# Cross-attention on one Trainium2 core: GpSimd issues the merge of the rest tiles behind the second addition of the next step instead of the first

## The chip, the cores and the metric

The kernel runs on one core of one Trainium2 chip. The metric is the device time of one execution in microseconds. The kernel is written engine by engine: TensorE (PE in the profile, its weight loads PEld), VectorE (DVE), ScalarE (ACT), GpSimd (POOL) and SyncE (SP) each run their own program, and semaphores order them.

## The reference

Cross-attention with grouped queries, on 4 batches of 1024 queries and 1601 keys, width 1024, 32 query heads, 8 key heads (4 query heads share one), head width 32:

```python
q = hidden_state @ Wq + bq          # (4, 1024, 1024)
k = encoder_hidden_state @ Wk + bk  # (4, 1601, 256)
v = encoder_hidden_state @ Wv + bv
scores = einsum('bkgld,bksd->bkgls', q, k) * scale + encoder_attention_mask
attn = softmax(scores, axis=-1)
out = einsum('bkgls,bksd->bkgld', attn, v)
x = out @ Wo + bo + hidden_state
return (x - mean(x)) * rsqrt(var(x) + 1e-6) * gamma + beta
```

Everything is float32. The mask is all zeros in these inputs; the kernel looks at a flag and takes the program without the mask.

## The kernel before

It has three stages with a barrier between them: `project` (queries, keys, values, written to DRAM), `attend`, and `output` (the last projection and the normalisation). The change is in `attend`.

**The steps of `attend`.** There are 64 steps: 8 blocks of 512 queries (`LQ`) by 8 key heads, each for the 4 query heads (`G`) that share a key head. A step has two halves which overlap with its neighbours'. For the *next* step TensorE computes scores with queries as rows (L882), and VectorE takes their maxima (L1027). For *this* step TensorE computes the scores again, transposed and with the maximum taken off (`logit`, L927), for 13 tiles (`ST`) of 128 keys by 4 heads, 52 in all; ScalarE takes their exponents (L1086) into a tile `weights` of 128 keys x 4 heads x 512 queries, 1 MiB; TensorE multiplies each tile with the values into `mixed` (L937).

**The denominators.** The sum of the exponents over all keys is taken in two parts. Nine tiles (`POOL` in the code: 0, 1, 3, 4, 6, 7, 9, 10, 12) are added by GpSimd, in 8 additions (`add`, L802), into `sum_pool`, one buffer for even and one for odd steps. The four others (`REST`: 2, 5, 8, 11) are added by DMAs that accumulate: `add_rest` (L813) adds tile 5, 8 or 11 into the buffer of tile 2. Then one more accumulating DMA, `merge` (L820), adds that buffer into `sum_pool`. All these DMAs are issued by GpSimd, in its own program's order, from one queue. Last, TensorE sums `sum_pool` over the keys with a matrix of ones (`denominators`, also L937, `logit<-sum_pool,ones` in the profile), ScalarE copies the result (L1104), and SyncE stores it. The denominators of step s are computed by TensorE in step s+1.

**The order around the change.** TensorE follows a string written out by hand (`ORDER`) in which each letter is one item: L a logit, S a half of scores, M a tile's mixing, T the turning of the maxima, P the denominators of the step before. P is the 62nd of 99 letters. What stands there waits for `rest_merged`, the merge's semaphore; everything behind it in the string waits with it. GpSimd's order is written in `sums`:

```python
for n in range(NPOOL):
    ...
    for k, st in enumerate(REST):
        if k and POOL[n] < st < POOL[n + 1]:
            add_rest(quad, s, k)
    add(quad, s, n)
    if n == 0 and not first:
        merge(quad * QUAD + (s - 1), s - 1)
```

An addition waits for the exponents of its tile and for the addition before it; `add_rest` for its tile's exponents and for the `add_rest` before it; `merge` for all additions and all rest additions of its step. In turn ScalarE, before it writes a tile, waits until the tile that last used the buffer has been mixed and added: the GpSimd tiles share 4 buffers, tiles 5, 8 and 11 share 2, tile 2 has 2 of its own, which are free when the merge of the step before last has landed.

**The last step** (63) has no scores of a next one. GpSimd leaves out the additions from tile 10 on and the last rest addition; TensorE sums tiles 10 to 12 itself. While it runs, SyncE loads what the output stage needs first: the weights `wo_parts` (L731) and the first `weighted` and `reciprocals` (L101, L106).

Of the kernel before, what the change touches and what calls it, by code (L numbers as in the profile page):

```python
# [527 lines left out]
def attend(nc, mask_flat, q_dram, k_dram, v_dram, a_dram, d_dram, r_dram, wo_dram, ident, flag, qk_store, qk_in, wo_in, mask_store, first_a, first_r, first_in):  # L528
# [14 lines left out]
    FIRST_ORDER = ORDER.replace("S", "SS", 2 * (LEAD - FIRST_LEAD))  # L543
    LO_AT = 24
    assert [ORDER.count(k) for k in "LSMTP"] == [ST * G, 2 * NROW, ST, 1, 1]
    BANKS = 3
    USES = [k for k in ORDER if k in "LTP"]
    assert len(USES) % BANKS == 0
    TURN, SUMS = USES.index("T"), USES.index("P")
# [8 lines left out]
    def bank_before(step, u):  # L558

        while True:  # L560
            u -= BANKS
            if u < 0:
# [10 lines left out]
    def buffer(s, st):  # L573

        if st == REST[0]:
            return s % BASES
        tiles, size, first = ring(st)
        return first + (s * len(tiles) + tiles.index(st)) % size
# [9 lines left out]
    with ExitStack() as held:  # L588
# [22 lines left out]
        score = [held.enter_context(nc.psum_tensor(f"score{i}", [P, 2, 512], F32)) for i in range(2)]  # L611
        logit = [held.enter_context(nc.psum_tensor(f"logit{i}", [P, LQ], F32)) for i in range(BANKS)]
        mixed = held.enter_context(nc.psum_tensor("mixed", [P, LQ], F32))
# [168 lines left out]
        @block.gpsimd  # L782
        def _(pool):

            nc.gpsimd.memset(ones[:], 1.0).then_inc(const_done, 1)
            for i, k in enumerate(k_sb[2:]):
                pool.wait_ge(const_done, 1 + i)
                nc.gpsimd.memset(k[STACK:SHIFT, :].bitcast(F32), 1.0).then_inc(const_done, 1)
            pool.wait_ge(const_done, 3)

            def add(quad, s, n):

                step, st = quad * QUAD + s, POOL[n + 1]
                w = min(P, S - st * P)
                pool.wait_ge(exp_done, quad * (QUAD * ST * G) + (s * ST + st + 1) * G)
                if n == 0:
                    pool.wait_ge(denom_done, step + 1)
                    first = weights[buffer(s, POOL[0])]
                else:
                    pool.wait_ge(pool_added, step * NPOOL + n)  # L800
                    first = sum_pool[s % 2]
                nc.gpsimd.tensor_tensor(sum_pool[s % 2][0:w], first[0:w], weights[buffer(s, st)][0:w], ALU.add).then_inc(pool_added, 1)  # L802

            def add_rest(quad, s, k):

                step, st = quad * QUAD + s, REST[k]
                pool.wait_ge(exp_done, quad * (QUAD * ST * G) + (s * ST + st + 1) * G)
                if k == 1:
                    pool.wait_ge(mix_done, quad * (QUAD * ST) + (s * ST + REST[0] + 1 + MIX0))
                else:  # L810
                    pool.wait_ge(rest_added, step * (16 * (len(REST) - 1)) + 16 * (k - 1))
                pool.sem_inc(pool_seen, 1)
                pool.dma_start(weights[buffer(s, REST[0])][:], weights[buffer(s, st)][:], accum_op=ALU.add).then_inc(rest_added, 16)  # L813

            def merge(step, s):

                pool.wait_ge(pool_added, step * NPOOL + NPOOL)
                pool.wait_ge(rest_added, step * (16 * (len(REST) - 1)) + 16 * (len(REST) - 1))
                pool.sem_inc(pool_seen, 1)
                pool.dma_start(sum_pool[s % 2][:], weights[buffer(s % QUAD, REST[0])][:], accum_op=ALU.add).then_inc(rest_merged, 16)  # L820

            def sums(quad, s, first=False, last=False):
                for n in range(NPOOL):
                    if last and POOL[n + 1] >= LATE:
                        break
                    for k, st in enumerate(REST):
                        if k and POOL[n] < st < POOL[n + 1]:
                            add_rest(quad, s, k)
                    add(quad, s, n)
                    if n == 0 and not first:  # L830
                        merge(quad * QUAD + (s - 1), s - 1)

            any_mask = pool.value_load(flag[0:1, 0:1], min_val=0, max_val=1)

            def clamp_max(a, lts):
                for lt in lts:
                    pool.wait_ge(mask_in[lt], a * 16 + 16)

                    pool.sem_inc(mask_max_seen, 1)
                    nc.gpsimd.tensor_scalar(mask_max[:, lt, :], mask_max[:, lt, :], -FAR, None, ALU.max).then_inc(mask_ready[lt], KVH // QUAD)  # L840

            def clamp_exp(a):
                pool.wait_ge(mask_exp_in, a * (16 * NLT) + 16 * NLT)

                pool.sem_inc(mask_exp_seen, 1)

                nc.gpsimd.tensor_scalar(mask_exp[:], mask_exp[:], -FAR, None, ALU.max).then_inc(mask_exp_ready, KVH // QUAD)

            def queries(a, first=False, final=False):
                with pool.If(any_mask > 0):  # L850
                    clamp_exp(a)
                for n in range(KVH):
                    if n >= KVH - 2 and not final:
                        with pool.If(any_mask > 0):
                            clamp_max(a + 1, range(0, 2) if n == KVH - 2 else range(2, NLT))
                    sums(a * (KVH // QUAD) + n // QUAD, n % QUAD, first and n == 0, final and n == KVH - 1)

            with pool.If(any_mask > 0):
                clamp_max(0, range(NLT))
            queries(0, first=True)  # L860
            for a in range(1, NLQ - 1):
                queries(a)
            queries(NLQ - 1, final=True)

        @block.tensor
        def _(pe):
# [20 lines left out]
            def bank_free(quad, s, u):  # L887

                step = quad * QUAD + s
                before = bank_before(step if isinstance(step, int) else QUAD + s, u)  # L890
                if before is None:
                    return
                if not isinstance(step, int):
                    before = before[0] - QUAD, before[1]
                    base = quad
                else:
                    base = 0
                bs, bu = before
                if USES[bu] == "L":
                    n = bs * (ST * G) + USES[:bu].count("L")  # L900
                    pe.wait_ge(exp_done, base * (QUAD * ST * G) + (n + 1))
                elif USES[bu] == "T":
                    pe.wait_ge(lo_copied, base * QUAD + (bs + 2))
                else:
                    pe.wait_ge(denom_copied, base * QUAD + bs)

            def turn(quad, s):
# [3 lines left out]
                if not (isinstance(step, int) and step == 0):  # L911
                    bank_free(quad, s - 1, TURN)
                nc.tensor.transpose(logit[TURN % BANKS][0:NROW, 0:P], row_max[s % 2][:].rearrange("p h t -> p (h t)"), ident[:]).then_inc(turn_done, 1)

            def logits(quad, s, u, masked):
# [9 lines left out]
                keys = slice(st * P, st * P + w)  # L925
                bank = logit[u % BANKS]
                last = nc.tensor.matmul(bank[0:w, :], k_sb[s][:, keys], q_sb[s][:, h, :], start=True, stop=not masked, skip_group_check=masked)  # L927
# [6 lines left out]
            def sum_heads(out, lhs, rhs, w, start, stop):  # L934

                for h in range(G):
                    last = nc.tensor.matmul(out[h * HD:(h + 1) * HD, :], lhs, rhs[0:w, h, :], start=start, stop=stop)  # L937
                return last
# [12 lines left out]
            def denominators(step, s):  # L951

                pe.wait_ge(rest_merged, step * 16 + 16)
                sum_heads(logit[SUMS % BANKS], ones[:], sum_pool[s % 2], P, True, True).then_inc(denom_done, 1)

# [447 lines left out]
```

## Time and profile before

| | us |
|---|---|
| median of 3 runs | 3845.93 |
| lowest, highest | 3843.28, 3846.05 |
| the profiled execution | 3848.16 |
| its span | 3846.5 |
| attention stage in it | about 810 to 3470 |
| PE, GpSimd busy in the span | 3776.4, 2888.6 |

The profile is of one execution. Its page gives for each engine the time in which it ran an instruction; a matrix product's end is modelled, so a busy PE may still be short of its best. A wait is put down to the event that came last before the waiting instruction began. A DMA is shown twice: as its issue on the engine that issues it, and by the time from there to its landing. Starts in the timelines are microseconds from the start of the span, and instructions of one kind in a row are merged, with "xN" for their number and their length together.

### The profile page before, as it was taken

The numbers are of one execution on the slowest core, as the hardware profiler recorded it, in microseconds if no ns is written. First come the engines' busy times: TensorE is split into PE (matmuls) and PEld (weight loads), VectorE is DVE, ScalarE is ACT, GpSimd is POOL, SyncE is SP. The second block draws the span as 40 slices with busy tenths as digits, with TensorE's granted clock in tenths as the row PEclk, the third lists the DMA queues.
The fourth block names the chain that finished last, engine by engine and source line by source line (L and its number), as shares of the span: only waits on it lengthen the run. The fifth ranks groups of instructions, "written<-read, shape, count | busy, mean of one in ns | idle before, by whom it ended". The sixth has DMA issues, their size and how long they took to land. (4 is left out here: it accounts for less than half of the span.)

```text
span 3846.5 us, 54629 instructions
## 1 busy us (share of the span) xinstructions
PE 3776.4 (98%) x20306; PEld 2381.8 (62%) x20306; DVE 2504.1 (65%) x2918; ACT 2034.1 (53%) x3865; POOL 2888.6 (75%) x1104
## 2 busy tenths in 40 slices
PE   8999999999999999999999999999999999999998
PEld 7998877755555555555555555555555555537886
DVE  3334555377777777777777777777777777735765
ACT  2222122136666666666666666666666666661110
POOL 1111111139999999999999999999999999994555
PEclk9999999979999999999999999999999999999999
DMA  5335677437667667767767667767767767667764
GB/s 177 136 139 181 222 264 249 156 65 157 146 143 158 146 144 154 149 143 158 146 144 157 145 144 156 148 143 156 147 143 157 146 145 156 152 163 212 203 190 125
DMA packets 297548, 612.08 MB, mean 159 GB/s; under 512 B 132064, under 2 KB 169056, under 8 KB 264800
## 3 DMA queue, kind: packets, MB, share of 16 engines
q0 software_dynamic: 58080, 337.15, 38.9%
q1 hardware_dynamic: 235968, 265.54, 26.1%
q10 hardware_dynamic: 3264, 6.29, 0.5%
q8 instruction: 142, 2.33, 0.2%
q14 instruction: 94, 0.77, 0.1%
HBM read 244.50 MB, written 96.99 MB: 89 GB/s over the span
## 5 line engine op out<-in xcount | busy, mean ns | idle before, releaser
L1027 DVE TENSOR_REDUCE half_max<-score 128x1 f32<-128x800 f32 (+1 forms) x2048 | 1893.4, 985 | 712.3 <-PE score L882 708.8
L1086 ACT ACTIVATE weights<-logit 128x512 f32<-128x512 f32 (+1 forms) x3328 | 1732.5, 603 | 801.2 <-PE logit L927 772.4
L802 POOL TENSOR_TENSOR sum_pool<-sum_pool,weights 128x2048 f32<-128x2048 f32 x446 | 2124.9, 4764 | 34.0 <-ACT weights L1086 6.4
L882 PE MATMUL score<-qk_store 96*128 96x400 f32 (+1 forms) x4096 | 1208.7, 377 | 14.0 <-issue 9.1
L927 PE MATMUL logit<-qk_store 98*128 98x512 f32 (+1 forms) x3328 | 1201.2, 417 | 7.6 <-ACT weights L1086 5.4
L882 PEld LDWEIGHTS score<-qk_store 96*128 96x128 f32 x4096 | 688.3, 191 | 551.1 <-DVE half_max L1027 424.9
L937 PE MATMUL mixed<-weights,v_sb 128*32 128x512 f32 x6656 | 809.9, 601 | 0.7 <-ACT weights L1086 0.7
L927 PEld LDWEIGHTS logit<-qk_store 98*128 98x128 f32 (+1 forms) x3328 | 607.9, 185 | 271.2 <-ACT weights L1086 135.8
L937 PEld LDWEIGHTS mixed<-weights,v_sb 128*32 128x32 f32 x6656 | 177.4, 109 | 393.7 <-ACT weights L1086 219.7
L802 POOL TENSOR_TENSOR sum_pool<-weights 128x2048 f32<-128x2048 f32 x64 | 313.6, 4900 | 49.4 <-ACT weights L1086 49.4
L514 POOL DMA_DIRECT2D q_parts<-o_hi x64 | 34.5, 539 | 311.5 <-DMA q_parts<-o_lo 214.5
L1234 PE MATMUL acc<-qk_store,a_hi 128*128 128x512 f32 x704 | 228.1, 397 | 6.1 <-DVE a_lo L1332 5.5
L377 ACT CAST t_hi<-turned 128x512 fp32r<-128x512 f32 x168 | 95.5, 585 | 143.2 <-PE turned L308 143.1
L813 POOL DMA_DIRECT2D weights<-weights x191 | 165.7, 868 | 5.7 <-issue 5.7
L399 ACT ACTIVATE o_hi<-summed,bq_scaled 128x512 fp32r<-128x512 f32 x64 | 44.0, 688 | 237.8 <-PE summed L313 147.1
L1234 PEld LDWEIGHTS acc<-qk_store,a_hi 128*128 128x128 f32 x704 | 133.0, 189 | 40.2 <-issue 7.5
L1234 PE MATMUL acc<-qk_store,a_lo 128*128 128x512 f32 x384 | 152.3, 397 | 0.0
L1370 POOL TENSOR_TENSOR total<-total,beta_row 128x1024 f32<-128x1024 f32 x32 | 96.2, 3007 | 70.8 <-DVE total L1322 70.8
L1363 POOL TENSOR_TENSOR total<-total,bo_row 128x1024 f32<-128x1024 f32 x32 | 88.3, 2764 | 78.6 <-DMA total<-in_x 78.4
L520 POOL DMA_DIRECT2D v_rows<-v_store x52 | 28.0, 539 | 157.1 <-DMA v_rows<-v_store 106.8
L424 DVE TENSOR_TENSOR t_lo<-turned,t_hi 128x512 fp32r<-128x512 f32 x168 | 113.1, 685 | 44.0 <-ACT t_hi L377 43.8
L468 DVE TENSOR_SCALAR full<-summed,bq_scaled 128x512 f32<-128x512 f32 x64 | 48.0, 750 | 143.0 <-ACT o_hi L399 143.0
(84 smaller groups left out, 2695.1 us busy)
## 6 DMA issues: line engine op xcount, KB each, us to landing
weights<-weights POOLq DMA_DIRECT2D x191, 1024.0 KB, 7.2
sum_pool<-weights POOLq DMA_DIRECT2D x63, 1024.0 KB, 7.0
qk_store<-q_parts SPq DMA_DIRECT2D x192, 256.0 KB, 3.9
qk_store<-k_parts SPq DMA_DIRECT2D x192, 200.1 KB, 5.6
rows<-in_ctx SPq DMA_DIRECT2D x26, 1024.0 KB, 5.2
landing<-in_mask_Bx1xSxS_ff SPq DMA_DIRECT2D x32, 800.5 KB, 7.1
rows<-in_x SPq DMA_DIRECT2D x16, 1024.0 KB, 6.3
q_parts<-o_hi POOLq DMA_DIRECT2D x64, 256.0 KB, 2.8
```

The costliest lines, as they stand in the source:

```text
L377: nc.scalar.copy(t_hi[par][:, t, :], turned[t % 2][:]).then_inc(hi_done, 1)
L424: nc.vector.tensor_tensor(t_lo[par][:, t, :], turned[t % 2][:], t_hi[par][:, t, :].bitcast(F32), ALU.subtract).then_inc(lo_done, 1)
L802: nc.gpsimd.tensor_tensor(sum_pool[s % 2][0:w], first[0:w], weights[buffer(s, st)][0:w], ALU.add).then_inc(pool_added, 1)
L813: pool.dma_start(weights[buffer(s, REST[0])][:], weights[buffer(s, st)][:], accum_op=ALU.add).then_inc(rest_added, 16)
L882: last = nc.tensor.matmul(score[j][:, c, 0:w], q_sb[buf][0:STACK, h, lt * P:(lt + 1) * P], k_sb[buf][0:STACK, start:start + w], start=True ...
L927: last = nc.tensor.matmul(bank[0:w, :], k_sb[s][:, keys], q_sb[s][:, h, :], start=True, stop=not masked, skip_group_check=masked)
L937: last = nc.tensor.matmul(out[h * HD:(h + 1) * HD, :], lhs, rhs[0:w, h, :], start=start, stop=stop)
L1027: nc.vector.tensor_reduce(half_max[m // NROW % 2][:, k % G, k // G, j:j + 1], score[j][:, :, 0:HALVES[j][2]], mybir.AxisListType.XY, ALU.m ...
L1086: nc.scalar.activation(weights[buffer(s, st)][0:w, h, :], logit[u % BANKS][0:w, :], ACT.Exp).then_inc(exp_done, 1)
L1234: last = nc.tensor.matmul(acc[j * NT + t][:, n, :], a[:, k, cols], w[k][:, out_cols], start=(k == 0 and m == 0), stop=(k == KVH - 1 and m ...
L1363: nc.gpsimd.tensor_tensor(total[r][:], total[r][:], bo_row[:], ALU.add).then_inc(resid_done, 1)
L1370: nc.gpsimd.tensor_tensor(total[r][:], total[r][:], beta_row[:], ALU.add).then_inc(final, 1)
```

## The change

`merge` is called behind the addition with n = 1 instead of n = 0. Everything else is the same text.

```diff
@@ -543,6 +543,7 @@
     FIRST_ORDER = ORDER.replace("S", "SS", 2 * (LEAD - FIRST_LEAD))
     LO_AT = 24
     assert [ORDER.count(k) for k in "LSMTP"] == [ST * G, 2 * NROW, ST, 1, 1]
+    MERGE_AT = 1
     BANKS = 3
     USES = [k for k in ORDER if k in "LTP"]
     assert len(USES) % BANKS == 0
@@ -827,7 +828,7 @@
                         if k and POOL[n] < st < POOL[n + 1]:
                             add_rest(quad, s, k)
                     add(quad, s, n)
-                    if n == 0 and not first:
+                    if n == MERGE_AT and not first:
                         merge(quad * QUAD + (s - 1), s - 1)
```

GpSimd, from the last addition of the first step (65 rows, tile 12) into the second. Its lines are numbered one higher after the change, since a line is added above them. The first addition of a step reads two tiles of weights (tiles 0 and 1), the second reads tile 3 (here `weights5`). Before:

```order
L802 TENSOR_TENSOR sum_pool1<-weights3,weights4 128x2048 [waits denom_done,exp_done]
L820 DMA sum_pool0<-weights0 128x2048 [waits pool_added,rest_added]
L802 TENSOR_TENSOR sum_pool1<-sum_pool1,weights5 128x2048 [waits pool_added,exp_done]
L802 TENSOR_TENSOR sum_pool1<-sum_pool1,weights2 128x2048 [waits pool_added,exp_done]
L813 DMA weights1<-weights7 128x2048 [waits exp_done,mix_done]
L802 TENSOR_TENSOR sum_pool1<-sum_pool1,weights3 128x2048 [waits pool_added,exp_done]
L802 TENSOR_TENSOR sum_pool1<-sum_pool1,weights4 128x2048 [waits pool_added,exp_done]
L813 DMA weights1<-weights6 128x2048 [waits exp_done,rest_added]
L802 TENSOR_TENSOR sum_pool1<-sum_pool1,weights5 128x2048 [waits pool_added,exp_done]
```

With the change:

```order
L803 TENSOR_TENSOR sum_pool1<-weights3,weights4 128x2048 [waits denom_done,exp_done]
L803 TENSOR_TENSOR sum_pool1<-sum_pool1,weights5 128x2048 [waits pool_added,exp_done]
L821 DMA sum_pool0<-weights0 128x2048 [waits pool_added,rest_added]
L803 TENSOR_TENSOR sum_pool1<-sum_pool1,weights2 128x2048 [waits pool_added,exp_done]
L814 DMA weights1<-weights7 128x2048 [waits exp_done,mix_done]
L803 TENSOR_TENSOR sum_pool1<-sum_pool1,weights3 128x2048 [waits pool_added,exp_done]
L803 TENSOR_TENSOR sum_pool1<-sum_pool1,weights4 128x2048 [waits pool_added,exp_done]
L814 DMA weights1<-weights6 128x2048 [waits exp_done,rest_added]
L803 TENSOR_TENSOR sum_pool1<-sum_pool1,weights5 128x2048 [waits pool_added,exp_done]
```

The merge (`sum_pool0<-weights0`) has gone behind the addition of tile 3, and stands one addition instead of two ahead of the next rest addition (`weights1<-weights7`). It is the same in every later step.

GpSimd in the last step; its merge is that of step 62. Before:

```order
L802 TENSOR_TENSOR sum_pool0<-sum_pool0,weights4 65x2048 [waits pool_added,exp_done]
L802 TENSOR_TENSOR sum_pool1<-weights5,weights2 128x2048 [waits denom_done,exp_done]
L820 DMA sum_pool0<-weights0 128x2048 [waits pool_added,rest_added]
L802 TENSOR_TENSOR sum_pool1<-sum_pool1,weights3 128x2048 [waits pool_added,exp_done]
L802 TENSOR_TENSOR sum_pool1<-sum_pool1,weights4 128x2048 [waits pool_added,exp_done]
L813 DMA weights1<-weights7 128x2048 [waits exp_done,mix_done]
L802 TENSOR_TENSOR sum_pool1<-sum_pool1,weights5 128x2048 [waits pool_added,exp_done]
```

With the change:

```order
L803 TENSOR_TENSOR sum_pool0<-sum_pool0,weights4 65x2048 [waits pool_added,exp_done]
L803 TENSOR_TENSOR sum_pool1<-weights5,weights2 128x2048 [waits denom_done,exp_done]
L803 TENSOR_TENSOR sum_pool1<-sum_pool1,weights3 128x2048 [waits pool_added,exp_done]
L821 DMA sum_pool0<-weights0 128x2048 [waits pool_added,rest_added]
L803 TENSOR_TENSOR sum_pool1<-sum_pool1,weights4 128x2048 [waits pool_added,exp_done]
L814 DMA weights1<-weights7 128x2048 [waits exp_done,mix_done]
L803 TENSOR_TENSOR sum_pool1<-sum_pool1,weights5 128x2048 [waits pool_added,exp_done]
```

Here too the merge has changed places with the addition behind it. The other engines' programs are the same.

## Rows read from the trace of the kernel before

**Rows 1.** The page: busy time and share of the span; busy tenths in 40 slices.

```profile
PE 3776.4 (98%) x20306; PEld 2381.8 (62%) x20306; DVE 2504.1 (65%) x2918; ACT 2034.1 (53%) x3865; POOL 2888.6 (75%) x1104
...
POOL 1111111139999999999999999999999999994555
```

**Rows 2.** The waits of ScalarE: line, releaser, us in total, times, longest.

```profile
ACT weights L1086 <- POOL sum_pool L802: 5.2, 1, 5.2
```

**Rows 3.** Groups by form, the merge: busy us, mean ns, idle before it, releasers.

```profile
L820 POOL DMA_DIRECT2D sum_pool<-weights x63 | 57.2, 908 | 45.3 <-DMA weights<-weights 36.1 <-POOL sum_pool L802 6.3 <-issue 2.8
```

**Rows 4.** The merge's own line, L820: who waited for it, and its landing.

```profile
  PE logit L937: 0.3, 1
...
DMA to landing us min/median/max: 6.9/7.0/9.2
```

**Rows 5.** TensorE in order of time, start and length, at two denominators.

```profile
1629.06 1.06 PE L937 MATMUL logit<-sum_pool,ones 128*32 128x512 f32 x8
...
1670.29 1.06 PE L937 MATMUL logit<-sum_pool,ones 128*32 128x512 f32 x8
```

**Rows 6.** GpSimd in order of time, one step and its two ends.

```profile
1608.84 4.92 POOL L802 TENSOR_TENSOR sum_pool<-sum_pool,weights 65x2048 f32<-65x2048 f32 x1
1613.37 4.92 POOL L802 TENSOR_TENSOR sum_pool<-weights 128x2048 f32<-128x2048 f32 x1
1617.96 1.16 POOL L820 DMA_DIRECT2D sum_pool<-weights  x1
1618.57 9.91 POOL L802 TENSOR_TENSOR sum_pool<-sum_pool,weights 128x2048 f32<-128x2048 f32 x2
...
1648.72 0.87 POOL L813 DMA_DIRECT2D weights<-weights  x1
...
1653.84 4.90 POOL L802 TENSOR_TENSOR sum_pool<-weights 128x2048 f32<-128x2048 f32 x1
1659.22 0.87 POOL L820 DMA_DIRECT2D sum_pool<-weights  x1 [0.48 <-POOL sum_pool L802]
1659.82 9.63 POOL L802 TENSOR_TENSOR sum_pool<-sum_pool,weights 128x2048 f32<-128x2048 f32 x2
1669.40 0.87 POOL L813 DMA_DIRECT2D weights<-weights  x1
```

**Rows 7.** The rest additions' line, L813: landing, minimum, median, maximum.

```profile
DMA to landing us min/median/max: 6.9/7.2/15.3
```

**Rows 8.** SyncE's DMA issues in order of time, the same step.

```profile
1645.96 1.39 SPq L91 DMA_DIRECT2D qk_store<-q_parts  x3
...
1651.07 4.75 SPq L667 DMA_DIRECT2D v_sb<-v_rows  x1
```

**Rows 9.** Two stretches of that step: busy us by engine, clock, DMA share, GB/s.

```profile
1658.00:1662.50 4.50, 4.50 (x29) 2.39 (x28) 2.94 (x5) 2.53 (x6) 4.02 (x3) 1.00 0.87 189
1662.50:1669.40 6.90, 6.90 (x38) 4.08 (x38) 5.32 (x7) 4.87 (x10) 6.76 (x3) 1.00 0.48 97
```

**Rows 10.** ScalarE in order of time, the same step.

```profile
1654.54 4.19 ACT L1086 ACTIVATE weights<-logit 128x512 f32<-128x512 f32 x8 [1.91 <-PE logit L927]
```

**Rows 11.** SyncE's issues at the end of the attention stage.

```profile
3410.06 0.44 SPq L101 DMA_DIRECT2D mask_store<-weighted  x1
```

**Rows 12.** GpSimd in order of time at the end of the attention stage.

```profile
3428.16 0.87 POOL L813 DMA_DIRECT2D weights<-weights  x1 [5.68 <-issue]
...
3433.23 4.86 POOL L802 TENSOR_TENSOR sum_pool<-weights 128x2048 f32<-128x2048 f32 x1
3437.71 1.22 POOL L820 DMA_DIRECT2D sum_pool<-weights  x1
```

**Rows 13.** TensorE in order of time in the last step.

```profile
3434.32 3.83 PE L927 MATMUL logit<-qk_store 98*128 98x512 f32 x7 [3.50 <-ACT weights L1086]
...
3445.13 1.07 PE L937 MATMUL logit<-sum_pool,ones 128*32 128x512 f32 x8 [0.26 <-DMA sum_pool<-weights]
```

**Rows 14.** A stretch of the last step, columns as above.

```profile
3434.00:3441.00 7.00, 6.68 (x23) 2.61 (x23) 0.00 (x0) 4.89 (x10) 7.00 (x3) 0.52 0.45 90
```

## The prediction

> **What bounds the kernel now.** I read the page first, then the waits, then one step of each engine in order of time, and last the end of the attention stage. The page [rows 1] shows TensorE (PE) busy 98% of the span. GpSimd (POOL) is busy 9 tenths in every slice of the attention stage, so it is the other candidate. The waits decide between them. Through ScalarE (ACT) GpSimd could slow PE, because the exponents need free weight buffers; ScalarE waited for an addition of GpSimd once, 5.2 us [rows 2]. PE waited for the merge once, 0.3 us [rows 4]. GpSimd itself stood 45.3 us before the merges, 36.1 of it for the DMA of the last rest tile [rows 3], some 0.7 us for each of 63. So PE sets the pace, and GpSimd keeps up with little to spare. One step lasts 41.23 us: the sum over heads that opens the denominators starts at 1629.06 and again at 1670.29 [rows 5].
>
> GpSimd's own work in a step comes from its timeline [rows 6]. Two additions and the issue behind them take 10.2 us (1659.82 to 1669.40, and 0.6 from an issue to what follows it), three times, 30.5. The last addition takes 4.5 until the next begins (1608.84 to 1613.37). The first addition with a merge that waits for nothing takes 5.2 (1613.37 to 1618.57). That is 40.2 us. GpSimd has 1.0 us of room in a step, and its wait at the merge uses most of it.
>
> **What the change does, part by part.** It adds and removes no instruction. In each of 63 steps the merge goes behind one addition more, and that addition (tile 3) goes ahead of it.
>
> 1. *The wait at the merge goes.* The last rest tile is issued at 1648.72 and the merge goes out at 1659.22 [rows 6], 10.5 us later, where a rest addition lands in 7.2 us in the median [rows 7]; the queries, issued at 1645.96, and what follows them on SyncE's queue share the DMA engines then [rows 8]. The new place is some 3 us behind that, so nothing is waited for there. What is late next is tile 3: its addition needs four exponents, the last of which is the sixth of the eight that start at 1654.54 [rows 10], so it ends 5 x 0.52 + 0.6 = 3.2 us later, at 1657.7. GpSimd, no longer held at 1659.2, and with 1.0 us of room per step to catch up, begins that addition at about 1657.8 instead of 1659.82. The 45.3 us of waiting turn into waits for ScalarE. Gain on the path: **nothing**, since nobody waits for GpSimd in these steps; if it did set the pace, all 45.3 us would be gained (rival C).
>
> 2. *The merge comes later.* It is issued behind that addition: 1657.8 + 4.6 (its duration: 9.63 for a pair [rows 6], of which the first takes 4.9 and a gap of 0.1) = 1662.4 instead of 1659.22. It lands 7.0 us later in the median, 6.9 to 9.2 over all [rows 4]: at 1669.4. PE reaches the denominators at 1670.29, with no wait ahead of them [rows 5]. The room shrinks from 4.1 us (1659.22 + 7.0 = 1666.2) to **0.9 us**. For the landing I take 7.0, not 9.2, because the stretch into which it moves is quiet: the DMA share falls from 0.87 before 1662.5 to 0.48 after [rows 9], and SyncE's small packets of the value rows, issued from 1651.07 over 4.75 us [rows 8], lie before today's merge and farther from the new one. The cost is then 0 in 62 steps; the far end is a landing of 9.2 in every step, 1.3 x 62 = 81 us.
>
> The Trainium skill, page DMA: Bandwidth & Descriptors, section "Anatomy of one DMA — SWDGE (gpsimd) path", gives such a transfer as 2.0 us plus its bytes at 436 GB/s, an estimate of 4.4 us for 1 MiB. This case's trace does not agree: 7.0 us in the median. By the page's figure the room would be 3.5 us and the wait of part 4 about 2.2 us, a sum of 3850.2 instead of 3853.1.
>
> 3. *What stands behind the moved issue.* The first rest addition now follows the merge by one addition, 5.2 us, where it was two, 10.2. It goes out at about 1667.6, before the merge has landed, and its bytes queue behind the merge's: it lands at about 1669.4 + 7.2 = 1676.6, as it does now (1669.40 + 7.2). It is waited for by the next rest addition, issued 10.2 us behind it, and by the exponents of tile 11, the earliest of which comes 28 exponents after 1657.7, at 0.79 us each (41.23 / 52): 1679.8. Both have over 1 us. SyncE's queue passes nothing: its store of the denominators follows PE's sum. Nothing is lost there. The last rest addition of a step may go out 1 us earlier and mix with the next queries and keys, which are loaded three steps ahead: nothing.
>
> 4. *The last step is different, and here I see a cost.* In step 62 the first loads of the output stage (at 3410.06, [rows 11]) come beside the rest additions, one of which takes 15.3 us to land [rows 7]; GpSimd stands 5.68 us, and then runs late: its first addition of the last step begins at 3433.23 [rows 12]. The merge is issued at 3437.71, and PE, which came to the denominators at 3444.87, waits 0.26 us until 3445.13 [rows 13]; so this merge took 7.4 us to its release. With the change the second addition goes first; both are over at 3433.23 + 9.6 = 3442.8, and the merge releases PE 7.0 to 7.4 us later, at 3449.8 to 3450.2. PE waits 5.0 to 5.4 us, less the 0.26 of now: **+4.9 us**. No scores are left to compute in that step; mixing and the last logits stand behind the denominators in PE's program, and the output stage behind those, so I let all of it through. The lower end is 0: if GpSimd's earlier start in step 62 gets its transfer in ahead of the loads, the 5.68 us and with them ScalarE's 5.2 shrink. The upper end adds the clock: after PE's gap of 3.50 us before 3434.32 [rows 13] the granted clock is 0.52 from 3434 to 3441 [rows 14], mostly the 1.2 GHz level, and another such 7 us would cost up to 3.4.
>
> **The sum**, against the profiled execution of 3848.16 us (its span is 3846.5): 0 + 0 + 0 + 4.9 = 3853.1. The median of the runs, 3845.93, lies 2.2 below the profiled one, so the forecast is 3850.8. That is 0.13% more; 0.2%, about what a measurement of this kernel can tell from no change, is 7.7 us.
>
> **The rivals.**
> *A. The room of 0.9 us is not there, and PE waits in every step.* For it: the room comes from one step's rows, and from a GpSimd that runs at the exponents' heels. If it stays where it is (first addition over at 1658.74), the merge goes out at 1663.3 and lands at 1670.3: no room at all. Two transfers in flight in one queue are also new. Against: 1.0 us per step to catch up, and the quiet stretch. It decides from a landing of 7.9 us on. With stalls between 0 and 9.2 - 7.0 = 2.2 us, most of them near 0, I take 0.4 us in 62 steps: 25 us, with the tail 3851 + 25 = 3876; the far end is 3932. Chance 0.18.
> *B. The tail costs more, by the clock*: 4.9 + 3.4 = 8.3, so 3854.2. For it: the 0.52 of [rows 14]. Against: such stretches are there already and may only change their place. Chance 0.10. The Trainium skill, page TensorE: Matmul & The Clock Gate, section "HAM oscillation — how this bites in real kernels", says that waits for a DMA bring the slower clock back; the row of 0.52 agrees.
> *C. GpSimd set the pace after all*, and its 45.3 us come off: 3800.6, faster. For it: it has no other idle time. Against: the single wait of [rows 2]. Chance 0.03.
> *D. Nothing changes at all*, because the transfers of step 62 fall out otherwise and the tail's two effects cancel: 3846. Chance 0.14.
>
> **How the numbers follow.** The forecast, no cost in the steps and 3 to 6 us at the end, has 0.55; with A to D this makes 1. The range takes in D (3844) and, above, B and the mildest of A (3863), and leaves out C and most of A, under 0.2 together. Within 0.2% (3838.2 to 3853.6) lie the forecast and D, 0.69, less 0.03 for a tail at its upper end, and 0.02 of a mild A: 0.68. Slower by over 0.2%: 0.28 + 0.03 - 0.02 = 0.29. Faster: 0.03.
>
> **What the changed profile would show.** Right: no wait of GpSimd at the merge's line; some 45 to 65 us of its waiting for exponents instead; steps of 41.2 us still; one wait of PE for the merge, some 5 us long, near 3445. Wrong: many short waits of PE for the merge (A), a merge that lands more than 7.9 us behind its issue, or steps shorter than 41.2 us (C).

## The result and the profile after

The changed kernel takes 3856.82 us (median of 12 runs, 3854.37 to 3860.98); the kernel before took 3846.39 in 12 runs on the same chip. The ratio is 1.0026, with an interval from 1.0017 to 1.0035: slower by 10.4 us, more than the 4.9 us of the forecast.

The page of the changed kernel, with the lines that answer to [rows 1] (lines of the program below the change are numbered one higher):

```profile
span 3855.5 us, 54629 instructions
...
PE 3776.7 (98%) x20306; PEld 2383.0 (62%) x20306; DVE 2505.5 (65%) x2918; ACT 2034.5 (53%) x3865; POOL 2885.2 (75%) x1104
...
POOL 1111111249999999999999999999999999994555
```

The span grew by 9.0 us and PE's busy time by 0.3. So the time went into gaps of PE. The waits of PE name them (columns as in [rows 2]), where there had been one wait of 0.3 us:

```profile
PE logit L938 <- DMA sum_pool<-weights: 12.3, 8, 6.7
...
PE logit L938 <- ACT weights L1087: 3.2, 4, 0.8
```

GpSimd did what the forecast said. Its groups, against [rows 3], show no wait of the merge for a rest tile any more but one (45.3 us before, one wait of 4.0 now). Before the dependent additions there are 87.7 us of idle time where there were 34.0, half of the 87.7 for ScalarE's exponents. The kernel before, then the change:

```profile
L802 POOL TENSOR_TENSOR sum_pool<-sum_pool,weights 128x2048 f32<-128x2048 f32 x383 | 1816.6, 4743 | 34.0 <-ACT weights L1086 6.4 <-PE mixed L937 0.4
...
L803 POOL TENSOR_TENSOR sum_pool<-sum_pool,weights 128x2048 f32<-128x2048 f32 x383 | 1833.4, 4787 | 87.7 <-ACT weights L1087 48.2 <-DMA weights<-weights 20.6 <-POOL sum_pool L803 0.4
...
L821 POOL DMA_DIRECT2D sum_pool<-weights x63 | 54.8, 870 | 4.0 <-issue 4.0
```

Nor did anyone else begin to wait long for GpSimd. ScalarE's row, against [rows 2], is longer but its longest wait is 0.4 us:

```profile
ACT weights L1087 <- POOL sum_pool L803: 18.0, 48, 0.4
```

In a step GpSimd now runs like this (start, length; step 5; compare [rows 6]):

```profile
1037.88 4.60 POOL L803 TENSOR_TENSOR sum_pool<-sum_pool,weights 128x2048 f32<-128x2048 f32 x1 [0.89 <-DMA weights<-weights]
1042.41 0.88 POOL L821 DMA_DIRECT2D sum_pool<-weights  x1
1043.02 4.89 POOL L803 TENSOR_TENSOR sum_pool<-sum_pool,weights 128x2048 f32<-128x2048 f32 x1
1047.55 1.19 POOL L814 DMA_DIRECT2D weights<-weights  x1
```

The merge goes out 15.9 us into the step (the step's first exponent starts at 1026.5; all places in a step are counted from there), as worked out: 1662.4 in the forecast's step is 16.0. TensorE's denominators follow, steps 4, 5, 6, 10, 15, 20 and the last, against [rows 5] and [rows 13]:

```profile
1009.12 1.06 PE L938 MATMUL logit<-sum_pool,ones 128*32 128x512 f32 x8
...
1051.67 1.06 PE L938 MATMUL logit<-sum_pool,ones 128*32 128x512 f32 x8 [1.26 <-DMA sum_pool<-weights]
...
1092.89 1.07 PE L938 MATMUL logit<-sum_pool,ones 128*32 128x512 f32 x8
...
1258.66 1.07 PE L938 MATMUL logit<-sum_pool,ones 128*32 128x512 f32 x8 [0.80 <-ACT weights L1087]
...
1465.46 1.06 PE L938 MATMUL logit<-sum_pool,ones 128*32 128x512 f32 x8 [0.60 <-DMA sum_pool<-weights]
...
1672.47 1.06 PE L938 MATMUL logit<-sum_pool,ones 128*32 128x512 f32 x8 [0.65 <-DMA sum_pool<-weights]
...
3453.38 1.94 PE L938 MATMUL logit<-sum_pool,ones 128*32 128x512 f32 x8 [6.72 <-DMA sum_pool<-weights]
```

From 1009.12 to 1051.67 are 42.55 us, from there to 1092.89 again 41.22. Over the whole stage eleven steps before the last one have a gap at the denominators, 0.54 to 1.27 us long and 8.8 us together: steps 5, 10, 15, 20, 26, 31, 36, 41, 52, 57 and 62. In the others PE finds the merge landed, or waits under 0.1 us. Where the row names ScalarE, the merge's landing decided all the same: the one issued at 1249.87 took 8.7 us, to 1258.6, and PE went on at 1258.66.

The balance of the two profiled executions, from the first exponent of a step to that of another, in us:

| | before | after |
|---|---|---|
| steps 1 to 61 | 2514.67 | 2524.40 |
| steps 62 and 63, to the last exponent | 84.2 | 86.4 |
| step 0 | 49.68 | 51.09 |
| to the first exponent | 813.7 | 810.5 |
| from the last exponent to the end | 384.2 | 383.2 |

The last three differ by -2.8 together, and the change touches none of them: the first merge is issued in step 1, and in the runs below, but for the one with added instructions, the first exponent comes anywhere from 808 to 815. The change itself is +9.7 in the steps, nearly all of it in the steps with a gap, and +2.2 at the end.

### Why a merge is late in one step of five

The landing of the merge of step 5 and of step 6, minimum, median and maximum of the single transfer, on its own line:

```profile
DMA to landing us min/median/max: 9.1/9.1/9.1
```

```profile
DMA to landing us min/median/max: 6.9/6.9/6.9
```

The DMA queues from the issue to PE's start, first for step 5, then for step 6 (queue, kind: packets, MB, share of 16 engines):

```profile
q0 software_dynamic: 206, 1.56, 85.2%
q8 instruction: 1, 0.02, 0.6%
```

```profile
q0 software_dynamic: 176, 1.31, 81.8%
```

In step 5 there is one packet of the instruction queue, 16 KB, in that window; in step 6 none. Packet by packet, it begins 7.0 us after the issue and takes 0.9. In steps 10, 15, 20 such a packet begins 5.2 to 6.5 us after the issue, too. The merge's semaphore is raised sixteen times, and in step 5 fifteen of these updates come 6.8 to 6.9 us after the issue and only the last one at 9.1; in step 6 all sixteen come by 6.9. So one sixteenth of the transfer is late, and PE waits for it. That the packet has to do with it was an idea from a coincidence; the experiment with padding below tests it.

The packet is not the whole reason. In the kernel before, 16 of the merges in steps 1 to 62 also have such a packet, 6.5 to 7.2 us behind their issue, among them those of all eleven steps above. Fifteen of them landed in 7.0 to 7.7 us and one in 9.2. In all, three of its 63 merges took longer than 7.9 us (7.97, 8.15 and 9.17); of the change's merges twelve did. In the change, too, steps 21 and 47 have a packet 6.8 and 7.2 us behind the issue, and their merges landed in 7.2 and 7.6 us. Most of the late landings came with the new place; they were not old ones that the smaller room laid bare. What it is about the new place is not shown. One thing that differs is the first rest addition, which GpSimd now issues 5.2 us behind the merge into the same queue, where it was 10.2; no run separates it from the packet.

### The last step

GpSimd, SyncE and the landing of the transfer that GpSimd issued at 3427.60 (it is the last rest addition of step 62); compare [rows 11] and [rows 12]:

```profile
3427.60 0.87 POOL L814 DMA_DIRECT2D weights<-weights  x1
...
3437.74 4.57 POOL L803 TENSOR_TENSOR sum_pool<-sum_pool,weights 128x2048 f32<-128x2048 f32 x1
3446.32 0.87 POOL L821 DMA_DIRECT2D sum_pool<-weights  x1 [4.01 <-issue]
```

```profile
3418.62 0.44 SPq L101 DMA_DIRECT2D mask_store<-weighted  x1
3419.11 5.36 SPq L106 DMA_DIRECT2D mask_store<-reciprocals  x4
3424.60 1.61 SPq L718 DMA_DIRECT2D reciprocals<-dens  x1
3426.26 0.91 SPq L732 DMA_DIRECT2D qk_store<-wo_parts  x1
```

```profile
DMA to landing us min/median/max: 18.2/18.2/18.2
```

GpSimd was ahead of its old place when the output stage's loads began at 3418.62. So an earlier rest addition had landed in time, and ScalarE's wait of 5.2 us is gone. But the next one, issued at 3427.60, came behind those loads and the 1.5 MB of projection weights issued at 3426.26, and took 18.2 us. The merge waited 4.01 us for it, went out at 3446.32 and kept PE until 3453.38, 6.72 us.

### The profile page after: what moved, and what is told of

The parts are those of the page before. It is cut to its first block and busy times, and to the rows that moved or that the text cites. A ratio compares the mean times of both kernels' runs of the same rounds, so it can differ in the third digit from the quotient of the medians.

```text
span 3855.5 us, 54629 instructions
## 1 busy us (share of the span) xinstructions
PE 3776.7 (98%) x20306; PEld 2383.0 (62%) x20306; DVE 2505.5 (65%) x2918; ACT 2034.5 (53%) x3865; POOL 2885.2 (75%) x1104
## 5 line engine op out<-in xcount | busy, mean ns | idle before, releaser
L803 POOL TENSOR_TENSOR sum_pool<-sum_pool,weights 128x2048 f32<-128x2048 f32 x446 | 2142.2, 4803 | 87.7 <-ACT weights L1087 48.2
L938 PE MATMUL mixed<-weights,v_sb 128*32 128x512 f32 x6656 | 810.5, 601 | 0.7 <-ACT weights L1087 0.7
L814 POOL DMA_DIRECT2D weights<-weights x191 | 186.1, 974 | 0.0
```

## The experiments

**1. The denominators later, in the changed kernel.** One letter of TensorE's order moves; the arithmetic is the same.

```diff
-... LLSLPMMLSLSLLL ...
+... LLSLMMPLSLSLLL ...
```

> The changed kernel, with TensorE's denominators (letter P) moved behind the two mixings that followed them, 1.9 us later in each step. Theory 1 (TensorE now reaches the denominators 0.9 us after a normal merge has landed, and in every fifth step or so a 16 KB packet of another DMA queue lets the merge land 1.3 us later, so it stalls 0.7 to 1.3 us there): the room becomes 2.8 us, the 12 long steps go back to 41.22 us (9.7 us less), the tail's wait of 6.7 us shrinks by 1.9; 3845 us, and GpSimd's order stays as in the change. Theory 2 (the change costs through what the later merge does to the rest additions and to ScalarE's buffers, not through the denominators' wait): about 3856 us, long steps stay.

Measured: 3845.91 us, ratio to the kernel before 0.9998 (0.9989 to 1.0007). Steps 1 to 61 take 2514.82 us, as before the change, and of PE's waits for the merge one is left, the last step's:

```profile
PE logit L938 <- DMA sum_pool<-weights: 4.5, 1, 4.5
```

The merge is issued at the same place as in the change (15.9 us into the step). So its lateness costs through the wait at the denominators and through nothing else that a run can tell. Theory 2 falls. The merges themselves land as late as in the change (8.4 to 9.2 us in the same eleven steps); they find 1.9 us more room.

**2. The same move in the kernel before.** The diff is the same, on the kernel before.

> Control for the run before: the kernel before, with the same move of the denominators behind two mixings. No step of it waits for the merge, so both theories expect no change in the steps; at most 0.3 us less in the last step. 3846 us. If it is faster or slower by over 3 us, the move has a price of its own, which is then taken off the other run.

Measured: 3847.06 us, ratio 1.0001 (0.9992 to 1.0010). The move has no price of its own, so the 10.9 us between run 1 and the changed kernel are the wait's. PE's gaps at the denominators agree: 15.5 us together in the change's profile, 4.5 in run 1's.

**3. The later merge in the last step alone.**

```diff
-                    if n == MERGE_AT and not first:
+                    if n == (MERGE_AT if last else 0) and not first:
```

> The merge goes behind the second addition in the last step alone. Theory 1: all steps but the last as before (no long ones), the last as in the change, 2 to 5 us more than before: 3848 to 3851 us. If most of the cost is in the tail: 3855 us.

Measured: 3849.82 us, ratio 1.0012 (1.0003 to 1.0021); steps 1 to 61 take 2514.68. TensorE in the last step:

```profile
3429.11 3.74 PE L928 MATMUL logit<-qk_store 98*128 98x512 f32 x7 [2.81 <-ACT weights L1087]
...
3444.55 1.94 PE L938 MATMUL logit<-sum_pool,ones 128*32 128x512 f32 x8 [4.45 <-DMA sum_pool<-weights]
```

This is the forecast's own case: GpSimd as late as before in step 62, the exponents waited for (2.81 us here), and one addition more ahead of the merge. PE's wait is 4.45 us, and steps 62 and 63 take 89.4 us, 5.2 more than before. The median of the runs rose by less, from 3846.96 to 3849.82 us, 2.9, inside the 2 to 5 expected.

**4. The later merge in all steps but the last.**

```diff
-                    if n == MERGE_AT and not first:
+                    if n == (0 if last else MERGE_AT) and not first:
```

> The merge goes behind the second addition in every step but the last. Theory 1: ten to twelve steps of 41.8 to 42.6 us, the others 41.22, 9 to 10 us more than before, and a tail without the wait of 6.7 us: 3853 to 3856 us. If most of the cost is in the tail: 3848 us.

Measured: 3856.39 us (6 runs), ratio 1.0032 (1.0020 to 1.0044). Steps 1 to 61 take 2523.57 us, 8.9 more than before, with the same long steps 5, 10, 15, ...; steps 62 and 63 take 83.9, as before, although PE waits 1.37 us for the last merge, which GpSimd had held back 7.61 us for a rest addition that took 17.6. Nearly all of the change's cost is in the steps. The costs in the profiles of runs 3 and 4 do not add up to the change's: in run 3 the tail costs 5.2 us, in the change 2.2, since there GpSimd comes into step 62 earlier.

**5. The merge behind the third addition.** `MERGE_AT = 2`.

> The merge behind the third addition, another 5.2 us later. Theory 1 (room of 0.9 us): TensorE waits 5.2 - 0.9 = 4.3 us at the denominators in each of 62 steps, period 45.5 us, 265 us more than the changed kernel without its long steps: about 4112 us; more, if the granted clock falls as well after each wait (it was 0.52 for 7 us after a gap of 3.5 us). Theory 2 (the cost is elsewhere): the steps grow by far less than 4 us.

Measured: 4251.88 us, ratio 1.106 (1.1043 to 1.1076). PE's waits and the granted clock (the mean of the whole span):

```profile
PE logit L938 <- DMA sum_pool<-weights: 247.4, 63, 5.9
```

```profile
core 0: 4247.3 us, clock 0.940
```

63 waits of 3.9 us, where 4.3 were worked out from a room of 0.9. The room was right: in the change the merge of step 10 landed after 8.7 us and PE waited 0.80, so 7.9 would have been free, 0.9 above the median. The later place was mis-sized: the merge goes out 20.6 us into the step, 4.7 and not 5.2 later than in the change, since one addition more stands ahead of it but no issue (0.6 us) more. 4.7 - 0.9 = 3.8 is what most of the waits are. But a step grew by 6.5 us, to 47.8: the rest is the clock, which stood at its lower level for 410 us of the attention stage, at 1.2 instead of 2.4 GHz. At half speed these cost up to 205 us, an estimate; 398 us for steps 1 to 61 less 61 x 3.9 leaves 160. The waits of the change itself, 0.5 to 1.3 us, did not bring the clock down.

**6. 98 instructions ahead of TensorE's attention program.** The counter is read by nobody.

```diff
+                for _ in range(98):
+                    pe.sem_inc(padding, 1)
                 steps(False)
```

> The changed kernel with 98 semaphore increments, used by nobody, ahead of TensorE's attention program. TensorE's program has 463 instructions a step by the trace, and 16 KB packets come in 1.8 times a step; if these are its code, 256 instructions each, the place of a packet in a step shifts by 49 instructions from step to step, which gives a coincidence every 5.2 steps, and 98 instructions more shift the long steps by two: from 5, 10, 15, 20, 26, 31, 36, 41, 52, 57 to about 7, 12, 17, 22, 28, 33, 38, 43, 54, 59. The time stays at 3857 us and up to 6 us for the increments. If the packets have nothing to do with the long steps, or are another engine's code, the steps 5, 10, 15, ... stay the long ones.

The number behind it: in the trace TensorE has 229 matrix products, 229 weight loads and 5 other instructions in a step, 463 in all. The instruction queue's row of the kernel before, for 62.5 steps of attention, is

```profile
q8 instruction: 113, 1.85, 0.3%
```

113 packets, 1.81 in a step; 463 / 256 is 1.81 too. Measured, the gaps at the denominators in TensorE's timeline, the first five:

```profile
906.14 1.07 PE L939 MATMUL logit<-sum_pool,ones 128*32 128x512 f32 x8 [0.74 <-ACT weights L1090]
...
1154.41 1.06 PE L939 MATMUL logit<-sum_pool,ones 128*32 128x512 f32 x8 [0.87 <-DMA sum_pool<-weights]
...
1361.32 1.06 PE L939 MATMUL logit<-sum_pool,ones 128*32 128x512 f32 x8 [0.76 <-ACT weights L1090]
...
1568.07 1.06 PE L939 MATMUL logit<-sum_pool,ones 128*32 128x512 f32 x8 [0.70 <-DMA sum_pool<-weights]
...
1774.92 1.06 PE L939 MATMUL logit<-sum_pool,ones 128*32 128x512 f32 x8 [0.57 <-DMA sum_pool<-weights]
```

These are steps 1, 7, 12, 17 and 22, and it goes on with 28, 33, 38, 43, 54 and 59: every one of the ten forecast, to the step, and step 1 beside them. So it is the place in TensorE's own program that picks the long steps, and they are steps in which a packet of its code comes during the merge's transfer. That such a packet alone does not make a merge this late was said above.

The time of this kernel, 3875 us in the one run, has 18 us more than the change. The increments took 0.15 us each, more than the 6 us expected for all of them, and stand in PE's idle time before its first score products of the stage; this run, then the change:

```profile
790.19 1.68 PE L884 MATMUL score<-qk_store 96*128 96x400 f32 x4 [23.97 <-issue]
```

```profile
769.75 1.70 PE L883 MATMUL score<-qk_store 96*128 96x400 f32 x4 [9.09 <-issue]
```

That is 14.9 us. The other 5 us or so of the later start lie ahead of it, in the first stage, where the starts of all runs scatter by some 7 us.

**7. The denominators only one mixing later.** `LLSLMPMLSLSLLL`.

> The changed kernel with the denominators behind only one of the two mixings, 0.95 us later: TensorE reaches them at 24.8 us into the step, and the latest merges are landed at 15.9 + 8.3 + 0.4 = 24.6. Theory 1: no long step of the series 5, 10, 15, ... is left, or some of at most 0.2 us. If the long steps come from something else than the landing of the merge, they stay.

Measured: 3849.16 us in one run. Three gaps are left in the steps, in 5, 26 and 31, beside 5.81 us in the last step:

```profile
1054.30 1.06 PE L938 MATMUL logit<-sum_pool,ones 128*32 128x512 f32 x8 [0.26 <-DMA sum_pool<-weights]
...
1920.29 1.07 PE L938 MATMUL logit<-sum_pool,ones 128*32 128x512 f32 x8 [0.31 <-DMA sum_pool<-weights]
...
2126.84 1.06 PE L938 MATMUL logit<-sum_pool,ones 128*32 128x512 f32 x8 [0.25 <-DMA sum_pool<-weights]
```

So the expectation was not quite met: the latest merges are later than the 8.3 + 0.4 us that I had put in. The 9.1 us on the merge's line above (step 5) ends at 1051.5, 25.0 us into the step, 0.2 behind the new place of the denominators. 0.95 us of room more takes away eight of eleven gaps and shortens the others.

**8. The output stage's first loads one step later, in the changed kernel.**

```diff
-                        if final and n == KVH - 2:
+                        if final and n == KVH - 1:
                             load_first()
```

> The changed kernel; SyncE's loads of the first weighted values and reciprocals for the output stage are issued one step later, at the end of step 63 instead of 62. If they are what holds up the last rest addition of step 62 (17.8 us to land), this one lands in 7 to 12 us, the merge goes out 15.9 us into step 63 and TensorE's wait of 6.7 us there is gone or under 1 us: 6 us less, 3851 us. If the loads of the weights of the output projection hold it up, nothing changes in the tail: 3857 us.

Measured: 3853.69 us, ratio 1.0020 (1.0011 to 1.0029). GpSimd at the end, and the landing of the transfer of 3425.76:

```profile
3425.76 0.88 POOL L814 DMA_DIRECT2D weights<-weights  x1
...
3435.93 4.55 POOL L803 TENSOR_TENSOR sum_pool<-sum_pool,weights 128x2048 f32<-128x2048 f32 x1
3440.44 0.85 POOL L821 DMA_DIRECT2D sum_pool<-weights  x1
```

```profile
DMA to landing us min/median/max: 10.5/10.5/10.5
```

The last rest addition lands in 10.5 us instead of 18.2, the merge goes out 16.4 us into the last step instead of 20.4 and waits for nothing, and PE's wait there is 1.06 us. Steps 62 and 63 take 80.3 us instead of 86.4. These loads, not the projection's weights alone, held it up. The median fell by 3 us, half of the 6 expected; in this profile steps 1 to 61 took 2525.8 us, 1.4 more than in the change's, so part of the rest is scatter between executions.

**9. The same in the kernel before.**

> The kernel before with the same later loads. The rest addition that took 15.3 us lands in 7 to 12, GpSimd's 5.7 us and ScalarE's 5.2 us of waiting are gone: 5 us less, 3841 us; if the output stage now waits for these loads instead, no change.

Measured: 3846.46 us, ratio 0.9999 (0.9990 to 1.0008): no gain. ScalarE's wait for GpSimd in the last step fell from 5.2 to 2.0 us, the rest addition of 15.3 us took 7.0, and still steps 62 and 63 take 84.9 us. The trace shows where it went: the loads, now issued from 3442.98, fall beside a rest addition of step 63, issued at 3443.46, which takes 12.6 us, and ScalarE waits for that one instead:

```profile
3456.11 3.55 ACT L1086 ACTIVATE weights<-logit 128x512 f32<-128x512 f32 x7 [5.67 <-DMA weights<-weights]
```

PE in turn waits 5.76 us for these exponents, where before the move it had waited 3.50 us in the same step [rows 13].

**10. Both remedies.** The diffs of runs 1 and 8 together, in the changed kernel.

> The changed kernel with both remedies: the denominators behind the two mixings, and the first loads of the output stage one step later. If the two costs found so far (long steps and the wait in the last step) are all there is, it has no long steps, no wait of over 1 us for the merge in the last step, and steps 62 and 63 together take 81 us instead of the 84.2 of the kernel before: 3 to 4 us less than before, 3843 us. If the later merge has a further cost, it stays at 3846 us or above.

Measured: 3844.49 us, ratio 0.9996 (0.9987 to 1.0005). Steps 62 and 63 take 81.3 us, as expected, no step is long, and PE waits for no merge; but from the last exponent to the output stage's first product are 12.6 us instead of 10.9, so more than half of the 3 us is given back. Most of that is a wait of PE, for a last rest addition that took 14.6 us beside the moved loads:

```profile
3463.17 1.07 PE L938 MATMUL logit<-weights,ones 128*32 128x512 f32 x8 [1.47 <-DMA weights<-weights]
```

3 to 4 us less were expected, and the time can't be told from the kernel before. No version tried beats that one.

## Why the prediction was right or wrong

**The number and the mechanism** part here. 3856.8 us lies in the range, but only because the range took in the mild form of rival A; the forecast itself was 3850.8, made of nothing in the steps and 4.9 us at the end, and the profiles show 9.7 and 2.2. That the range held is luck as far as the forecast's mechanism goes. Slower by over 0.2%, which is what was measured (1.0026), had a chance of 0.29 against 0.68 for no such difference. Two of the prediction's own signs of being wrong are in the trace: several short waits of PE for the merge, and merges that land more than 7.9 us behind their issue.

**The bound** was read rightly. PE sets the pace, and 45.3 us of GpSimd's waiting were worth nothing when they went. Steps without a late merge take 41.22 us in both kernels.

**Part 1** held: no merge waits for its rest tiles, but in the last step. GpSimd's idle time before the dependent additions grew by 53.7 us to 87.7. The part of it put down to exponents went from 6.4 to 48.2, up by 41.8, a little under the 45 to 65 named; 20.6 are put down to a DMA.

**Part 2** is the step that failed. The issue (15.9 us into the step against 16.0), the normal landing (6.9 to 7.0 us) and PE's arrival were right, so in 51 of 62 steps the cost was 0. But the part took the median landing for every step, "because the stretch into which it moves is quiet". The DMA share and SyncE's timeline don't show instruction fetches, and in eleven steps the merge landed 8.4 to 9.1 us behind its issue. Against a room of 0.9 us above the median that costs 0.5 to 1.3 us each time. The term was put at 0 and measured 9.7 us. The far end of the row before would not have given it either: only three of its 63 landings were over 7.9 us, by 1.6 us together. The step took the landings of the old place for those of the new one. Rival A named what may be the missing part, two transfers in flight in one queue; whether it is stays open.

**Part 3** held for the rest additions themselves: with the denominators moved (run 1) nothing is left of a cost, though the first rest addition is issued before the merge has landed. It did not ask what that rest addition does to the merge ahead of it, which is the question left open above.

**Part 4** had the mechanism and the size of its own case: +4.9 forecast, +5.2 in run 3's profile (+2.9 in its median). In the full change the tail costs 2.2 us, by a longer wait of PE (6.7) and a vanished one of ScalarE (5.2). The text named the second as a lower end, but not that the next rest addition would be caught by the same loads.

**The rivals.** A happened in a thinner form: PE waits, from a landing of about 8 us on, as it said; but in one step of five, 0.16 us a step in the mean and not 0.4. The clock (B) did fall at PE's wait of 6.72 us: it stood at its 1.2 GHz level from 3447.2, half a microsecond into the wait, to 3457.5 (eight products of the denominators took 1.94 us instead of 1.07). But it stood there for 13.7 us between 3413 us and the stage's end in both kernels, in other places, so no longer than before, as the text had held against this rival. Neither GpSimd as the pace (C), nor no change at all (D) came true. In the profiles the steps' 9.7 and the tail's 2.2 make 11.9; the median of the runs moved by 10.4.

## What to carry to other kernels

When a transfer is moved toward the one that waits for it, compare the room that is left with its late landings, not with the median, and ask how often they come: with 0.9 us of room, one late landing in five steps cost 0.5 to 1.3 us each. And don't take the old place's landings for the new one's: here three of 63 were over 7.9 us before and twelve after, so ask what else is in the queue and on the engines there. A wait that disappears on an engine that does not set the pace is no gain, and the order behind it may have been cheap protection. Loads that are moved out of the way of one transfer can hold up the next: in runs 9 and 10 the moved loads met a later rest addition, and the gain went again, all of it or half. Where late landings come at a regular count of steps, look for something that has another period than the step, such as the program's own code.

## What the runs showed of the hardware

- TensorE's instructions come in 16 KB packets on a queue of their own, which the profile counts among the same 16 DMA engines that move the data: 113 in 62.5 steps of 463 instructions, one for every 256. Each takes 0.9 to 1.7 us.
- In the change, merges of 1 MB with such a packet 4.6 to 7.1 us behind their issue landed in 8.4 to 9.1 us instead of 6.9 in eleven cases and in 7.2 in one; one sixteenth of the transfer is late, the others are not. In the kernel before, with a packet 6.5 to 7.2 us behind, fifteen of sixteen landed in 7.0 to 7.7 us.
- 98 increments of a semaphore by TensorE, one behind the other, cost 0.15 us each in run 6.
- An accumulating transfer of 1 MB, 6.9 us at its best, took 15.3 and 18.2 us beside loads that SyncE had issued.
- Waits of 3.9 us in each step of 48 left TensorE's clock at its 1.2 GHz level for 410 us; waits of up to 1.3 us in one step of five did not.
